# One stretch of turns, values and scores in a fused attention and recurrent-gate kernel

## The chip, the cores and the metric

The kernel runs on one core of a Trainium2 chip. The metric is device time in microseconds (us): 938.83 us, the median of 3 runs (937.73 to 939.91). The core's engines are TensorE (PE; its weight loads are PEld), VectorE (DVE), ScalarE (ACT), GpSimd (POOL) and SyncE (SP), which issues nearly all DMAs. Each works through its own list of instructions in order, and semaphores tie them together.

## The reference

The input x is 8 x 512 x 512, and so is the context. Two residual blocks follow each other:

```python
# block 1: windowed attention; queries = layernorm(x), keys = values = context
scores = einsum(q, k) / sqrt(32)          # 16 heads of 32
scores = where(|i - j| > 64, -inf, scores)
x = x + softmax(scores) @ v @ W_proj.T + b_proj
# block 2: a gated recurrence over the 8 batches, state of 512 x 512
f, i, g = sigmoid(x2 @ wf.T + c @ uf.T + bf), sigmoid(...), tanh(...)   # x2 = layernorm(x)
c = f * c + i * g
x = x + tanh(x2 @ wo.T + c_final @ uo.T + bo)
```

## The kernel before, in words

Rows are cut in 32 tiles of 128 (4 per batch; t is the tile's place in its batch, 0 to 3). A tile's 16 heads are 4 groups of 4, and one group of one tile is a slot: 128 slots. For a slot, TensorE computes scores (L753) into four PSUM banks `ps_a`, VectorE adds the mask and takes the row minimum (L1035, the mask step), ScalarE takes the exponential and its sum (L923), TensorE turns the part under the tile's own keys (L775) into a PSUM bank and ScalarE copies it out (L928, counted by `turned_a`), VectorE turns the sides in 32x32 blocks (L1070, step `sides`), and TensorE multiplies by the values (L796, L801) into `ps_v`. Edge tiles (t = 0 and 3) have half the sides.

Behind a tile's four slots come: `recip` (reciprocals of the sums, L1046), `send` (turned and sent through DRAM, L1051), `mult` (values by reciprocals, L1080), `halves` (split in a rounded part on ScalarE, L936, and a rest on GpSimd, L685), `proj` on TensorE into `ps_m` (L706 to L708), `resid` (L1085, empties `ps_m`), `stat2`, and `ln2b` (L1105). The normalised tile is turned for block 2: in tiles t = 3 by TensorE into `ps_m` (`turn2`, L843), in the others (`MOVED`, 18 tiles) by a DMA through DRAM and a block transpose on VectorE (`turn2`, L1111), with a rounded copy on ScalarE (`turn2_hi`, L945) and a rest on VectorE (`turn2_lo`, L1118). Queries of tiles from 11 on come as x_t by DMA (`load_q`, L580) and are normalised by VectorE in two operations (`query_norm`, L1025 and L1027).

Block 2's gate products are `cell`s: three matmuls of 128x512 each (L706 to L708 into `ps_g`), 8 cells to a unit. When a unit is whole, ScalarE takes its tanh (`gate`, L970), and VectorE blends it (L1142, L1156, L1159).

The order is one list, `steps`, written out by hand at L152 to L339; every engine walks through it and picks its own steps. From slot 36 on (`FIRST_TWO`) the slots go two by two: a double slot has two turns, 12 cells (2, 3 and 7), scores of the next two slots, and the values of its own two. Double slots with s = 0 also carry the projection of the tile before, and those with s = 2 the `mult` of their own. VectorE's `ln1` (L1003 to L1008) takes the statistics of tile i+2. Both turns go to `ps_a` banks, which is why the scores wait for both copies.

Of the kernel before, what the change touches and what calls it, by code (L numbers as in the profile page):

```python
# [20 lines left out]
def bass_xattn_ffn(nc, x, x_t, ctx_rows, ctx_t, w_proj, b_proj, w_gates, u_gates, biases, w_out, u_out, b_out, in_c,  # L21
# [143 lines left out]
    while cells_done < len(products):  # L165
        i, s = n // G, n % G
        if n >= FIRST_TWO:
            both = [m for m in (n, n + 1) if m < SLOTS]
            ahead = [m for m in (n + 2, n + 3) if m < SLOTS]
            steps.extend(("turn", m) for m in both)  # L170
            if s == 0:
                tile_steps("ln1", i + 2)
            cells(2)
# [6 lines left out]
            gates(2)  # L180
            steps.extend(("score", m) for m in ahead[:1])
            if s == 2 and i - 1 not in MOVED:
                tile_steps("turn2_lo", i - 1)
            steps.extend(("score", m) for m in ahead[1:])
            if s == 0:
# [6 lines left out]
            steps.extend(("exp", m) for m in ahead)  # L192
            steps.extend(("value", m) for m in both)
            if s == 0:
                tile_steps("proj", i - 1)
            else:
                tile_steps("mult", i)
            gates()
            renew()
            cells(3)  # L200
            steps.extend(("recip", m) for m in ahead[:1])
            if s == 0:
                tile_steps("resid", i - 1)
                tile_steps("stat2", i - 1)
            else:
                tile_steps("halves", i)
            steps.extend(("recip", m) for m in ahead[1:])
            if s == 0:
                tile_steps("send", i)
            steps.extend(("sides", m) for m in ahead[:1])  # L210
            if s == 0 and i + 1 >= TURNED_X:
                tile_steps("query_norm", i + 1)
            if s == 0 and i + 1 < TURNED_X:
                tile_steps("query", i + 1)
                tile_steps("query_out", i + 1)
            if s == 0 and i - 2 in MOVED:
                tile_steps("turn2", i - 2)
                tile_steps("turn2_hi", i - 2)
            gates()
            cells(7)  # L220
            if s == 0 and i - 1 not in MOVED:
                if i - 2 in MOVED:
                    tile_steps("turn2_lo", i - 2)
                tile_steps("ln2b", i - 1)
# [8 lines left out]
            gates(3)  # L233
            steps.extend(("sides", m) for m in ahead[1:])
            renew()
# [119 lines left out]
    with ExitStack() as ctx:  # L355
# [130 lines left out]
        x2t_home[0] = x2t_home[B - 2]  # L486
        ps_turn = [ps_g[0] if n < OWN_BANKS else ps_a[n % 2 if n >= FIRST_TWO else 0] for n in range(SLOTS)]

# [215 lines left out]
        def _(pe):  # L704
# [13 lines left out]
            for kind, i in steps:  # L718
# [14 lines left out]
                if kind == "score":  # L733
# [4 lines left out]
                    if i >= FIRST_TWO + 2:  # L738
                        pe.wait_ge(masked, HPG * (i - i % 2))
                        pe.wait_ge(turned_a, i - i % 2)  # L740
                    else:
                        need(pe, masked, HPG * i)
                        if i - 2 >= OWN_BANKS:
                            pe.wait_ge(turned_a, i - 1)
# [11 lines left out]
                if kind == "turn":  # L756
                    own = OWN0[i // G % TT]
                    if i < OWN_BANKS:
# [9 lines left out]
                        continue  # L768
                    if i >= FIRST_TWO:
                        pe.wait_ge(masked, HPG * (i - i % 2 + 2))  # L770
                    else:
                        pe.wait_ge(masked, HPG * (i + 1) + 1)
# [48 lines left out]
                if kind == "proj":  # L821
# [3 lines left out]
                    if i < WHOLE:  # L825
                        pe.wait_ge(attn_t, i + 1)
                        for k in range(G):
                            mm = pe.matmul(ps_m[:, :], attn[:, k, :], wp[:, k, :], start=(k == 0), stop=(k == G - 1))  # L828
                    else:
                        pe.wait_ge(wp_lo, G)  # L830
                        pe.wait_ge(attn_split, i - WHOLE + 1)
                        if i + 1 >= SENT:
                            pe.wait_ge(q_ready, min(i + 2, TURNED_X))
                        for k in range(G):
                            mm = product(ps_m[:, :], (attn_hi[:, k, :], attn_lo[:, k, :]),
                                         (proj_w[:, 0, k, :], proj_w[:, 1, k, :]), k == 0, k == G - 1)
                    mm.then_inc(projected, 1)
                if kind == "turn2" and i not in MOVED:
                    pe.wait_ge(x2_done, i + 1)
                    need(pe, q_ready, min(i + 3, TURNED_X))  # L840
                    need(pe, column_turned, len([n for n in row_at if n < G * (i + 1) + 2]))
                    for k in range(G):
                        mm = pe.transpose(ps_m[:, k * P:(k + 1) * P], x2[:, k * P:(k + 1) * P], ident[:, :])  # L843
# [59 lines left out]
        def _(act):  # L903
# [4 lines left out]
            for kind, i in steps:  # L908
# [16 lines left out]
                if kind == "turn":  # L925
                    act.wait_ge(turned, i + 1)
                    need(act, valued, i - i % 2 if i >= FIRST_TWO else i)
                    act.activation(own_home[i], ps_turn[i][:, :].rearrange("p (a q) -> p a q", a=HPG), ACT.Copy)\  # L928
# [65 lines left out]
        def _(dve):  # L994
# [4 lines left out]
            for kind, i in steps:  # L999
# [21 lines left out]
                if kind == "query_norm":  # L1021
# [5 lines left out]
                    dve.tensor_tensor(queries[:, :, :], queries[:, :, :], rstd, ALU.mult).then_inc(q_ready, 1)  # L1027
                if kind == "score":
                    t = i // G % TT
# [28 lines left out]
                if kind == "sides":  # L1058
                    dve.wait_ge(expd, HPG * (i + 1))
                    dve.wait_ge(valued, i - i % 2 if i >= FIRST_TWO else i)  # L1060

# [180 lines left out]
```

## Time and profile before

| | |
|---|---|
| median of 3 runs | 938.83 us (937.73 to 939.91) |
| profiled execution | 939.05 us, of which the span 937.2 |
| TensorE busy | 920.3 us, 98% of the span |
| VectorE busy | 674.9 us, 72% |
| ScalarE busy | 476.7 us, 51% |
| GpSimd busy | 206.0 us, 22% |
| granted TensorE clock, mean | 0.998 |

The table is read from the profile's first part. Busy time is the time in which an engine executes, without its waits; ends of matmuls are modelled, so on TensorE the distances between starts say more than the durations.

### The profile page before, as it was taken

The numbers are of one execution on the slowest core, as the hardware profiler recorded it, in microseconds if no ns is written. First come the engines' busy times: TensorE is split into PE (matmuls) and PEld (weight loads), VectorE is DVE, ScalarE is ACT, GpSimd is POOL, SyncE is SP. The second block draws the span as 40 slices with busy tenths as digits, with TensorE's granted clock in tenths as the row PEclk, the third lists the DMA queues.
The fourth block names the chain that finished last, engine by engine and source line by source line (L and its number), as shares of the span: only waits on it lengthen the run. The fifth ranks groups of instructions, "written<-read, shape, count | busy, mean of one in ns | idle before, by whom it ended". The sixth has DMA issues, their size and how long they took to land.

```text
span 937.2 us, 21983 instructions
## 1 busy us (share of the span) xinstructions
PE 920.3 (98%) x7842; PEld 716.2 (76%) x7842; DVE 674.9 (72%) x2275; ACT 476.7 (51%) x1430; POOL 206.0 (22%) x236
## 2 busy tenths in 40 slices
PE   7999899999999999999999999999999999999998
PEld 5555567677887788878787888788877888888887
DVE  6888987888779977997799878987798531143222
ACT  6888666655555544555465555555555321131222
POOL 5576322211111111111111111111101100003444
PEclk9999999999999999999999999999999999999999
DMA  9564223224443443434543444344333150059862
GB/s 303 165 200 145 86 80 108 87 69 130 132 139 112 130 132 92 143 108 129 133 141 109 119 116 125 108 109 109 98 99 92 50 164 0 1 178 384 316 233 101
DMA packets 139348, 123.58 MB, mean 132 GB/s; under 512 B 46824, under 2 KB 104168, under 8 KB 137704
## 3 DMA queue, kind: packets, MB, share of 16 engines
q1 hardware_dynamic: 138520, 121.91, 42.9%
q8 instruction: 63, 1.03, 0.5%
q10 hardware_dynamic: 720, 0.27, 0.2%
q14 instruction: 45, 0.37, 0.1%
HBM read 87.70 MB, written 34.46 MB: 130 GB/s over the span
## 4 chain that ended last, share of the span: by engine, by line
PE 89%; DVE 5%; ACT 2%; issue 2%; DMA 1%; SPq 0%; DVEq 0%; ACTq 0%
PE ps_g L706 18%; PE ps_g L708 18%; PE ps_g L707 18%; PE ps_a L753 5%; PE ps_a L775 5%; PE ps_m L706 3%; PE ps_v L796 3%; PE ps_m L708 3%; PE ps_m L707 3%; PE ps_m L828 2%; PE ps_a L708 2%; PE ps_a L706 2%; PE ps_a L707 2%; ACT probs L923 2%; PE ps_v L801 2%
## 5 line engine op out<-in xcount | busy, mean ns | idle before, releaser
L923 ACT ACTIVATE probs<-probs,rowmin 128x192 f32<-128x192 f32 (+1 forms) x512 | 239.4, 470 | 114.0 <-DVE rowmin L1035 114.0
L1035 DVE CUSTOM_DVE_ANT_0 probs<-ps_a,mask 128x192 f32<-128x192 f32 (+1 forms) x512 | 166.1, 386 | 28.4 <-PE ps_a L753 26.8
L706 PE MATMUL ps_g<-state_hi,gate_w 128*128 128x512 f32 x336 | 133.6, 398 | 0.0
L708 PE MATMUL ps_g<-state_hi,gate_w 128*128 128x512 f32 x336 | 131.1, 390 | 0.0
L707 PE MATMUL ps_g<-state_lo,gate_w 128*128 128x512 f32 x336 | 130.8, 389 | 0.0
L1070 DVE STREAM_TRANSPOSE keys<-probs 32x128 f32<-32x128 f32 x420 | 125.5, 299 | 5.6 <-issue 0.2
L970 ACT ACTIVATE gate<-ps_g,bias 128x512 f32<-128x512 f32 x84 | 57.6, 686 | 105.8 <-PE ps_g L708 105.1
L923 ACT ACTIVATION_READ_ACCUMULATOR probs<-probs,rowmin 128x1 f32 x512 | 96.4, 188 | 0.0
L928 ACT ACTIVATE probs_t<-ps_a 128x512 f32<-128x512 f32 x108 | 59.3, 595 | 61.1 <-PE ps_a L775 61.1
L685 POOL TENSOR_TENSOR attn_lo<-recip,attn_hi 128x512 fp32r<-128x512 f32 x23 | 29.7, 1292 | 275.8 <-ACT attn_hi L936 275.8
L706 PE MATMUL ps_g<-x2t_even,gate_w 128*128 128x512 f32 x192 | 80.5, 419 | 0.0
L706 PE MATMUL ps_g<-x2t_odd,gate_w 128*128 128x512 f32 x192 | 76.9, 401 | 0.0
L708 PE MATMUL ps_g<-x2t_even,gate_w 128*128 128x512 f32 x192 | 75.6, 394 | 0.0
L707 PE MATMUL ps_g<-x2t_even,gate_w 128*128 128x512 f32 x192 | 75.5, 393 | 0.0
L708 PE MATMUL ps_g<-x2t_odd,gate_w 128*128 128x512 f32 x192 | 74.9, 390 | 0.0
L707 PE MATMUL ps_g<-x2t_odd,gate_w 128*128 128x512 f32 x192 | 74.8, 390 | 0.0
L708 PEld LDWEIGHTS ps_g<-state_hi,gate_w 128*128 128x128 f32 x336 | 63.1, 188 | 13.5
L706 PEld LDWEIGHTS ps_g<-state_hi,gate_w 128*128 128x128 f32 x336 | 63.1, 188 | 12.6
L707 PEld LDWEIGHTS ps_g<-state_lo,gate_w 128*128 128x128 f32 x336 | 63.2, 188 | 12.3
L753 PE MATMUL ps_a<-keys,queries 32*64 32x192 f32 (+1 forms) x2048 | 62.7, 326 | 2.4 <-DVE rowmin L1035 1.9
L775 PE MATMUL ps_a<-ident,probs 128*128 128x128 f32 x432 | 60.5, 274 | 2.2 <-ACT probs L923 0.8
L775 PEld LDWEIGHTS ps_a<-ident,probs 128*128 128x128 f32 x432 | 51.1, 139 | 14.4 <-ACT probs L923 4.2
(220 smaller groups left out, 1723.5 us busy)
## 6 DMA issues: line engine op xcount, KB each, us to landing
values<-ctx_rows SPq DMA_DIRECT2D x34, 256.0 KB, 4.4
xr<-x SPq DMA_DIRECT2D x32, 256.0 KB, 3.8
keys<-ctx_t SPq DMA_DIRECT2D x16, 512.0 KB, 4.2
x_dram<-xr SPq DMA_DIRECT2D x32, 256.0 KB, 2.6
gate_w<-x2t_dram SPq DMA_DIRECT2D x8, 1024.0 KB, 10.1
keys<-ctx_t SPq DMA_DIRECT2D x16, 384.0 KB, 3.4
x2t_dram<-x2t_even SPq DMA_DIRECT2D x12, 512.0 KB, 4.4
x2t_dram<-x2t_odd SPq DMA_DIRECT2D x12, 512.0 KB, 4.5
```

What stands on the lines that cost most here:

```text
L685: pool.tensor_tensor(attn_lo[:, :, :], attn if i < SENT else recip[:, :, :], attn_hi[:, :, :].bitcast(F32), ALU.subtract)\
L706: pe.matmul(ps, lhs[0], rhs[0], start=start, stop=False)
L707: pe.matmul(ps, lhs[0], rhs[1], start=False, stop=False)
L708: return pe.matmul(ps, lhs[1], rhs[0], start=False, stop=stop)
L753: mm = pe.matmul(ps_a[h][q, score_at[i] + k.start:score_at[i] + k.stop], queries[rows, g, q], keys[rows, key_home[tile], g, k], start=True ...
L775: mm = pe.transpose(ps_turn[i][:, h * P:(h + 1) * P], probs[:, i % 2, h, own:own + P], ident[:, :])
L796: pe.matmul(ps_v[HEAD * h:HEAD * (h + 1), g * P:(g + 1) * P], values[:, tile % 2, 0, d], own_home[i][:, h, :], start=True, stop=False)
L923: act.activation(row, row, ACT.Exp, bias=rowmin[:, i % 2, h:h + 1], scale=-1.0, accum_out=rowsum[:, i // G % 2, i % G, h:h + 1]).then_inc( ...
L928: act.activation(own_home[i], ps_turn[i][:, :].rearrange("p (a q) -> p a q", a=HPG), ACT.Copy)\
L970: act.activation(gate[:, min(gt, 1), :], ps_g[i % 2][:, :], ACT.Tanh, bias=(first_bias if b == 0 else bias)[:, gt, m:m + 1], scale=1.0 if ...
L1035: dve.tensor_tensor_reduce(probs[:, i % 2, h, 0:SEEN[t]], ps_a[h][:, score_at[i]:score_at[i] + SEEN[t]], mask[:, MASK0[t]:MASK0[t] + SEEN[ ...
L1070: turn = dve.transpose(side_home[i][BLK * keys_of:BLK * (keys_of + 1), :, q], probs[q, i % 2, :, col:col + BLK])
```

## The change

From slot 36 on, TensorE's order in a double slot n, n+1 is: turn n, values n-2 and n-1, turn n+1, scores n+2 and n+3, and then the cells; before it was both turns, 2 cells, scores, values, 10 cells. Values come one double slot later than before. Odd turns go to `ps_m` in place of `ps_a[1]`, with waits for what else uses that bank; the scores wait only for the first turn's copy. On VectorE, scores' masks are a step of their own (`mask`), behind both `sides`; `query_norm` follows, then `ln1`, `recip`, `resid`, `stat2`, `send` and the `turn2` of a moved tile. `mult` and `halves` of a tile move to the start of the next double slot, the projection behind 5 cells, and the `query` of tile 10 behind all cells.

```diff
             both = [m for m in (n, n + 1) if m < SLOTS]
             ahead = [m for m in (n + 2, n + 3) if m < SLOTS]
-            steps.extend(("turn", m) for m in both)
-            if s == 0:
-                tile_steps("ln1", i + 2)
+            back = [m for m in (n - 2, n - 1) if FIRST_TWO <= m < SLOTS]
+            steps.extend(("turn", m) for m in both[:1])
+            steps.extend(("value", m) for m in back)
+            steps.extend(("turn", m) for m in both[1:])
+            steps.extend(("score", m) for m in ahead)
+            if s == 0 and i - 1 >= SENT:
+                tile_steps("mult", i - 1)
+                tile_steps("halves", i - 1)
+            late_sides = [m for m in both if m >= FIRST_TWO + 2]
+            steps.extend(("sides", m) for m in late_sides[:1])
             cells(2)
...
             gates(2)
-            steps.extend(("score", m) for m in ahead[:1])
+            steps.extend(("sides", m) for m in late_sides[1:])
             if s == 2 and i - 1 not in MOVED:
                 tile_steps("turn2_lo", i - 1)
-            steps.extend(("score", m) for m in ahead[1:])
+            steps.extend(("mask", m) for m in ahead)
...
             steps.extend(("exp", m) for m in ahead)
-            steps.extend(("value", m) for m in both)
-            if s == 0:
-                tile_steps("proj", i - 1)
-            else:
-                tile_steps("mult", i)
             gates()
             renew()
             cells(3)
-            steps.extend(("recip", m) for m in ahead[:1])
             if s == 0:
+                tile_steps("proj", i - 1)
+            gates()
+            if s == 0 and i + 1 >= TURNED_X:
+                tile_steps("query_norm", i + 1)
+            if s == 0:
+                tile_steps("ln1", i + 2)
+                steps.extend(("recip", m) for m in ahead)
                 tile_steps("resid", i - 1)
                 tile_steps("stat2", i - 1)
-            else:
-                tile_steps("halves", i)
-            steps.extend(("recip", m) for m in ahead[1:])
-            if s == 0:
                 tile_steps("send", i)
-            steps.extend(("sides", m) for m in ahead[:1])
-            if s == 0 and i + 1 >= TURNED_X:
-                tile_steps("query_norm", i + 1)
-            if s == 0 and i + 1 < TURNED_X:
-                tile_steps("query", i + 1)
-                tile_steps("query_out", i + 1)
             if s == 0 and i - 2 in MOVED:
                 tile_steps("turn2", i - 2)
                 tile_steps("turn2_hi", i - 2)
             gates()
             cells(7)
+            if s == 0 and i + 1 < TURNED_X:
+                tile_steps("query", i + 1)
+                tile_steps("query_out", i + 1)
...
             gates(3)
-            steps.extend(("sides", m) for m in ahead[1:])
+            if s == 2:
+                steps.extend(("recip", m) for m in ahead)
...
-        ps_turn = [ps_g[0] if n < OWN_BANKS else ps_a[n % 2 if n >= FIRST_TWO else 0] for n in range(SLOTS)]
+        ps_turn = [ps_g[0] if n < OWN_BANKS else ps_m if n >= FIRST_TWO and n % 2 else ps_a[0] for n in range(SLOTS)]
...  # TensorE, score
-                        pe.wait_ge(turned_a, i - i % 2)
+                        pe.wait_ge(turned_a, i - i % 2 - 1)
...  # TensorE, turn
+                        tile = i // G
                         pe.wait_ge(masked, HPG * (i - i % 2 + 2))
+                        if i % 2:
+                            pe.wait_ge(recip_out, SENT)
+                            pe.wait_ge(x1_done, tile - 1 + (i % G) // 2)
+                            pe.wait_ge(x2_lo, split_by(tile - 1))
+                            pe.wait_ge(q_ready, min(tile + 1 + (i % G) // 2, TURNED_X))
...  # TensorE, proj; turn2 has the same with + 4
+                            pe.wait_ge(turned_a, min(G * (i + 1) + 2, SLOTS))
...  # ScalarE, turn; VectorE, sides has the same
-                    need(act, valued, i - i % 2 if i >= FIRST_TWO else i)
+                    need(act, valued, i - 1 if i >= FIRST_TWO + 2 else i - i % 2 if i >= FIRST_TWO else i)
...  # VectorE
-                if kind == "score":
+                if kind == ("mask" if isinstance(i, int) and i >= FIRST_TWO + 2 else "score"):
```

## Rows read from the trace of the kernel before

**Rows 1.** Stretches view: engines' busy us and instructions, granted clock, DMA share, GB/s
```profile
195.00:730.00 535.00, 535.00 (x4921) 429.15 (x4920) 448.98 (x1538) 286.97 (x902) 83.07 (x84) 1.00 0.42 117
```
**Rows 2.** Timeline, TensorE: start, us, engine, line, operation, count; three stretches
```profile
505.07 1.03 PE L775 MATMUL ps_a<-ident,probs 128*128 128x128 f32 x8
...
519.03 1.03 PE L775 MATMUL ps_a<-ident,probs 128*128 128x128 f32 x8
519.82 0.48 PE L706 MATMUL ps_g<-x2t_even,gate_w 128*128 128x512 f32 x1
520.14 0.40 PE L707 MATMUL ps_g<-x2t_even,gate_w 128*128 128x512 f32 x1
...
521.05 0.39 PE L708 MATMUL ps_g<-x2t_even,gate_w 128*128 128x512 f32 x1
521.37 0.88 PE L753 MATMUL ps_a<-keys,queries 32*64 32x192 f32 x32
522.18 0.43 PE L796 MATMUL ps_v<-probs_t,values 128*32 128x128 f32 x8
...
523.19 0.50 PE L706 MATMUL ps_g<-x2t_even,gate_w 128*128 128x512 f32 x1
523.53 0.40 PE L707 MATMUL ps_g<-x2t_even,gate_w 128*128 128x512 f32 x1
...
554.71 1.03 PE L775 MATMUL ps_a<-ident,probs 128*128 128x128 f32 x8
...
568.37 1.03 PE L775 MATMUL ps_a<-ident,probs 128*128 128x128 f32 x8
```
**Rows 3.** Timeline, TensorE, before the double slots: turns ahead of values and of scores
```profile
72.08 0.66 PE L819 MATMUL ps_m<-ident,recip 128*128 128x128 f32 x4
72.66 0.78 PE L789 MATMUL ps_v<-probs_t,values 128*32 128x128 f32 x16
...
124.59 0.60 PE L731 MATMUL ps_m<-ident,tile_row 128*128 128x128 f32 x4
125.12 0.58 PE L753 MATMUL ps_a<-keys,queries 32*64 32x192 f32 x16
```
**Rows 4.** The load of x_t: DMA view, VectorE's waits (total, times, longest), two timelines
```profile
queries<-x_t SPq DMA_DIRECT2D x21, 256.0 KB, 4.3
...
DVE queries L1025 <- DMA queries<-x_t: 4.3, 7, 1.3
...
561.26 0.58 SPq L580 DMA_DIRECT2D queries<-x_t  x1
...
565.54 0.69 DVE L1025 TENSOR_TENSOR queries<-queries,tile_row 128x512 f32<-128x512 f32 x1 [0.60 <-DMA queries<-x_t]
```
**Rows 5.** Timeline, VectorE, in the double slot that starts at 505.07
```profile
508.68 0.69 DVE L1003 BATCH_NORM_STATS2 st<-xr 128x6 f32<-128x512 f32 x1
...
509.77 0.42 DVE L1035 CUSTOM_DVE_ANT_0 probs<-ps_a,mask 128x256 f32<-128x256 f32 x1
...
512.63 0.66 DVE L1085 TENSOR_TENSOR xr<-ps_m,xr 128x512 f32<-128x512 f32 x1
...
514.39 0.18 DVE L1046 RECIPROCAL invsum<-rowsum 128x4 f32<-128x4 f32 x1
...
514.74 1.84 DVE L1070 STREAM_TRANSPOSE keys<-probs 32x128 f32<-32x128 f32 x6
516.61 0.69 DVE L1025 TENSOR_TENSOR queries<-queries,tile_row 128x512 f32<-128x512 f32 x1
...
518.14 0.71 DVE L1111 STREAM_TRANSPOSE tile_row<-x2t_odd 128x512 f32<-128x512 f32 x1
```
**Rows 6.** Timeline, ScalarE, around the next turns
```profile
518.89 0.63 ACT L945 ACTIVATE x2t_odd<-tile_row 128x512 fp32r<-128x512 f32 x1 [3.96 <-DVE tile_row L1111]
519.43 0.67 ACT L970 ACTIVATE gate<-ps_g,bias 128x512 f32<-128x512 f32 x1
520.00 1.08 ACT L928 ACTIVATE probs_t<-ps_a 128x512 f32<-128x512 f32 x2
```

More of the change, by code:

```diff
@@ L841, in _ @@
                     need(pe, column_turned, len([n for n in row_at if n < G * (i + 1) + 2]))
+                    if i + 1 >= SENT:
+                        pe.wait_ge(turned_a, min(G * (i + 1) + 4, SLOTS))
                     for k in range(G):
@@ L1059, in _ @@
                     dve.wait_ge(expd, HPG * (i + 1))
-                    dve.wait_ge(valued, i - i % 2 if i >= FIRST_TWO else i)
+                    dve.wait_ge(valued, i - 1 if i >= FIRST_TWO + 2 else i - i % 2 if i >= FIRST_TWO else i)
                     if i == OWN_BANKS:
```

## The prediction

> **What bounds the kernel now.** I read the stretch view first, over the part of the span in which attention and the gate products run together in double slots: between 195 and 730 us TensorE is busy for all 535.00 us at a granted clock of 1.00 (its higher level, 2.4 GHz), VectorE for 449, ScalarE for 287 and GpSimd for 83 [rows 1]. So no wait of TensorE is there to be taken away; the time can fall only if TensorE starts its next group sooner, and it rises with every wait that is new. Then I read TensorE in order of time through one double slot [rows 2]. Only starts are used, since the ends are modelled: a gate product is three matmuls, each starting 0.227 us after the one before. I call the start of a double slot's first turn T0. Last I followed VectorE and ScalarE through the double slots that carry a projection (s = 0, below called A; the one after it, s = 2, is B) [rows 4 to 6], since 449 of 535 us is close to full for an engine that works strictly in the order written.
>
> **TensorE's own time.** The profiled double slot B has 36 gate matmuls, 36 x 0.227 = 8.17 us. The rest: eight turns 0.79 and the next matmul's longer first gap (0.32 instead of 0.23) 0.09; the gap ahead of the scores 0.32 instead of 0.23, so 0.09; 32 score instructions 0.81; the two slots' values 1.01; the first gap after them 0.34, so 0.11. Sum 2.90 us [rows 2]. Eight turns with the entry of what follows are 0.88, or 0.11 a turn: breaking the gate products for turns costs next to nothing.
>
> After the change the order is turn, values, values, turn, scores. Four turns ahead of values took 0.58 us, four ahead of scores 0.53 [rows 3]; against 4 x 0.11 = 0.44 that is 0.14 and 0.09 more. Values again 1.01, scores 0.81; what follows the scores is now a gate matmul, which the trace never shows; by its nearest rows its first gap is longer by 0.09 to 0.11 [rows 2], and the turn behind the values by as much. Sum 0.58 + 1.01 + 0.10 + 0.53 + 0.81 + 0.10 = 3.13 us, 0.2 more than before. Bounds: if a turn is as cheap ahead of values and scores as ahead of gate products (0.44 for four) and values cost the turn behind them nothing, the sum is 0.44 + 1.01 + 0.44 + 0.81 + 0.09 = 2.79 and the change gains 0.11 a double slot; if each of the two edges never seen (values to turn, scores to gate matmul) costs what the gap ahead of the scores and the one after values do together, 0.2, the sum is 3.33 and it loses 0.43. Near the middle but towards the cheap side I take a loss of 0.13, for 45 double slots (first slots 36 to 124) 6 us, range -5 to +19.
>
> The Trainium skill, TensorEngine Tiling (Array Packing), Key Properties, says that a change of tiling mode drains TensorE. Turns and gate products are both full 128x128, so by it there were three mode changes in a double slot (to scores, to values, back) and will be four (values, back to a turn, scores, back): the fewer stretches hold more drains. At 0.09 to 0.2 each that alone would be 4 to 9 us slower. The trace agrees in that the turn next to gate products is the one edge that is nearly free [rows 2].
>
> **The queue behind the queries.** Here is the large term. In A VectorE now does: `mult`, both `sides`, eight masks, `query_norm`, then `ln1`, two `recip`, `resid`, `stat2`, `send`, and only then VectorE's `turn2` of tile i-2. ScalarE's copy of it (`turn2_hi`) stands ahead of the gate that ends with A's last cell, and that ahead of the copy of B's first turn; and B's scores wait for that copy (`turned_a`), because they overwrite its bank. Before, `turn2` stood right behind `query_norm`, and the scores came two gate products later.
>
> `query_norm` can't come earlier, because x_t isn't there: its load is issued once the last scores of the tile are done, 4.9 to 6.5 us behind T0 in the trace (561.26 - 554.71 = 6.55 in the one shown) and lands a median 4.3 us later; VectorE stood waiting for it in 7 of 21 tiles, and in the one shown, with t=0, began at T0 + 10.83 [rows 2, 4]. The new order ends A's scores at T0 + 3.1, where they end now, so the landing stays: T0 + 10.9 for t=0, where one more value load is issued ahead of it, and for the others the request at 4.9 to 5.5 plus 4.3 and a little: some 9.8 for t=3 and 9.7 for t=2 (estimates). VectorE is free before that: `mult` from T0 + 1.9, sides 2 x 1.9, masks 2.8, so T0 + 9.2 at the latest.
> From the start of `query_norm`: until its successor starts 1.53; `ln1` 1.09; one `recip` 0.2 (estimate); `resid` and `stat2` 514.39 - 512.63 = 1.76; the other `recip` and `send` 0.35; so `turn2` starts 4.9 us behind it instead of 1.53 [rows 5]. From its start: ScalarE's copy after 0.75, gate after 1.29, the turn's copy after 1.86 and done at 2.4 to 2.5 [rows 5, 6]. Together 7.4 us from `query_norm` to the bank being free.
> When B's scores are due: A took 519.03 - 505.07 = 13.96 (t=2) and 568.37 - 554.71 = 13.66 (t=0) [rows 2], plus 0.13; the scores follow 0.6 + 1.0 + 0.6 = 2.2 behind that, at T0 + 16.3 and T0 + 16.0 (15.8 where an edge tile's short side values save 0.2, estimate).
> So the wait is 10.9 + 7.4 - 15.8 = 2.5 us at t=0 (5 tiles), 9.8 + 7.4 - 15.8 = 1.4 at t=3 (5), 9.7 + 7.4 - 16.3 = 0.8 at t=2 (6), none at t=1, whose tile i-2 is turned by TensorE. 12.5 + 7.0 + 4.8 = 24 us; I take 23, as t=2 is often nearer nothing. The bounds are 0 (should ScalarE or the load be 2 us earlier than laid out) and 40 (a microsecond more in each of 16). TensorE has no slack elsewhere to win it back.
>
> **Edits that I cost at nothing.** Odd turns go to `ps_m` and wait for `resid`, done at `query_norm` + 3.4, T0 + 13.2 to 14.3, while the turn is due at T0 + 15.6; where that cover is gone it costs what is missing. `mult` of a tile comes one double slot later and its halves are ready near T0 + 5; the projection has five gate products ahead of it now and starts at T0 + 3.1 + 3.4 = 6.5. The masks of A start near T0 + 6.5 instead of 4.7 and the exponentials end by T0 + 11, due at the next turn, T0 + 14; in B they end near its end, with 1 to 2 us to spare for the second turn. If that is gone too, each A loses about 1 us. SyncE: keys, values and x_t are requested at the same offsets; the tile's store and the send come 1 to 2 us later, in front of loads that are needed a double slot on. The later query of tile 10 happens once: under 1 us either way. Values a double slot later use sides and copies that are long done.
>
> Sum against the profiled execution's 939.05 us (span 937.2 and 1.85 around it): 939.05 + 23 + 6 = 968.05. It stands 0.22 above the median 938.83, so 967.8 us.
>
> **Rivals.** (1) The queue is not late, only the edges count: 939 + 6 = 945. For it: VectorE has 86 us idle in the stretch; against it: x_t's landing was already waited for. 20%. (2) The other side: the single stretch lets weight loads run ahead across edges, each double slot gains 0.11, as in the lower bound, and `turn2` is in time because masks and sides are out of the way: 939 - 45 x 0.11 = 934. It decides if a double slot's attention takes under 2.90 us on TensorE and x_t lands before T0 + 8.4. For it: two breaks of the gate products become one; against it: rows 2 to 4. 8%. (3) Both the queue and a second wait: in B the masks, behind two sides, let ScalarE's exponentials reach past T0 and push gate and copy in A too; 22 times 0.5 us more: 979. 14%. (4) It comes to nothing, edges cheaper and waits small: 939. 5%. The forecast, 23 us of waits and 6 of edges, has 53%, its own range 955 to 975.
>
> Slower by over 0.2% (about what can be told from no change here) is the forecast, rivals 1 and 3, and nothing else: 87%; same 4%, faster 9%. Range: from 943 (rival 1 inside) to 981 (rival 3 inside).
>
> **What would show it.** Right: TensorE idle ahead of the scores in B with ScalarE's `probs_t` copy as what ended it, about 2.5, 1.4 and 0.8 us at t=0, 3, 2 and nothing at t=1; VectorE idle ahead of L1025 for x_t in nearly every tile; in an unwaited double slot 3.0 to 3.1 us between gate products. Wrong: no TensorE idle between 195 and 750 us, or idle ahead of the turns instead of the scores; a stretch under 2.9 us.

## The result, and the profile after

The changed kernel takes 983.5 us, the median of 4 runs (982.62 to 988.8), against 938.7 us for the kernel before (4 runs, 937.73 to 939.91). The ratio is 1.0488, with a 95% interval of 1.0449 to 1.0528. The forecast was 967.8 us with a range up to 981: the direction is right, the time lies 2.5 us above the range. The profiled execution took 983.95 us with a span of 982.0 us, and the granted clock had a mean of 0.984 (before: 0.998).

The first part of the page after, and the chain of waits by engine (share of the span):

```profile
PE 940.0 (96%) x7842; PEld 730.1 (74%) x7842; DVE 652.5 (66%) x2275; ACT 477.3 (49%) x1430; POOL 199.9 (20%) x236
...
PE 59%; DVE 15%; DMA 11%; SPq 7%; issue 4%; ACT 4%; POOL 0%; ACTq 0%; DVEq 0%
```

Before, TensorE held the chain nearly alone; now 41% of it runs over other engines, the DMAs and SyncE's queue (SPq). The stretches view of after has first the whole part with double slots, then a piece of one B (t = 2), the one in the timeline below:

```profile
195.00:780.00 585.00, 558.56 (x4987) 445.44 (x4978) 433.12 (x1567) 289.76 (x912) 75.78 (x83) 0.98 0.39 107
...
548.90:552.90 4.00, 4.00 (x14) 3.13 (x11) 3.90 (x20) 1.32 (x6) 0.00 (x0) 0.50 0.87 266
```

TensorE was busy for every microsecond of the stretch of before [rows 1]; it is idle for 26.4 of these 585 us. The second line runs at half clock (0.50, which is 1.2 GHz); from 553.20 on the clock is 1.00 (2.4 GHz) again. The waits view (total us, times, longest) names what TensorE, VectorE and SyncE waited for in the same part:

```profile
PE ps_a L755 <- ACT probs_t L939: 26.0, 15, 2.9
DVE queries L1036 <- DMA queries<-x_t: 50.3, 18, 5.0
...
SPq L503 <- DMA x_dram<-tile_row: 50.7, 16, 5.1
```

The first line is the wait that was forecast: scores behind ScalarE's copy of the first turn. The second is VectorE's wait for x_t, 4.3 us in 7 times before [rows 4]. The last is SyncE waiting for the store of x2 to land.

TensorE in order of time (start, us, line, operation, count): the end of an A without a wait, and the B that follows it, with one.

```profile
527.78 0.60 PE L783 MATMUL ps_a<-ident,probs 128*128 128x128 f32 x4
528.32 0.43 PE L804 MATMUL ps_v<-probs_t,values 128*32 128x128 f32 x8
529.33 0.66 PE L783 MATMUL ps_m<-ident,probs 128*128 128x128 f32 x4
529.91 0.91 PE L755 MATMUL ps_a<-keys,queries 32*64 32x192 f32 x32
530.75 0.50 PE L708 MATMUL ps_g<-state_hi,gate_w 128*128 128x512 f32 x1
...
541.79 0.60 PE L783 MATMUL ps_a<-ident,probs 128*128 128x128 f32 x4
543.82 0.63 PE L783 MATMUL ps_m<-ident,probs 128*128 128x128 f32 x4 [0.42 <-issue]
547.39 1.56 PE L755 MATMUL ps_a<-keys,queries 32*64 32x192 f32 x32 [2.94 <-ACT probs_t L939]
548.88 0.80 PE L708 MATMUL ps_g<-x2t_even,gate_w 128*128 128x512 f32 x1
549.47 0.63 PE L709 MATMUL ps_g<-x2t_even,gate_w 128*128 128x512 f32 x1
549.90 0.63 PE L710 MATMUL ps_g<-x2t_even,gate_w 128*128 128x512 f32 x1
```

In A (527.78) the five groups stand close together: 0.54 + 1.01 + 0.58 + 0.84, and then a first gate gap of some 0.34. In B the scores start at 547.39, after 2.94 us idle. Behind that wait the 32 score instructions take 1.49 us in place of 0.84, and up to about 552.9 the matmuls start 0.43 us apart in place of 0.227.

**Where 44.8 us went.** From the start of the second double slot (206.05 us before, 205.10 after) to one and the same gate matmul behind the last (777.04 and 822.0) the trace of before has 570.99 us and that of after 616.9, so 45.9 us lie there; ahead of it after is 1 us quicker. They come apart like this: 26.4 us of idle time, 26.0 of it ahead of the scores of 15 double slots and 0.4 ahead of one second turn; 11.9 us in 7 stretches at half clock (8.2 of it in gate matmuls, 3.0 in scores, 0.6 in the rest, each taken against the same distance between starts at full clock); and what is left, 7.6 us, which I put down to the edges, 0.17 in each of 44 double slots. The starts in double slots without a wait give the same 0.17 by themselves: on average 0.53 + 0.61 for the turns, 0.83 for the scores and 0.11 for the longer first gate gap, 2.08 us, where before it was 0.79 + 0.09 + 0.09 + 0.83 + 0.11 = 1.91; the values are alike.

**Why ScalarE's copy is late.** VectorE and ScalarE in the double slots of the fence above (T0 of A is 527.78):

```profile
539.96 0.69 DVE L1036 TENSOR_TENSOR queries<-queries,tile_row 128x512 f32<-128x512 f32 x1 [2.82 <-DMA queries<-x_t]
...
544.84 0.68 DVE L1122 STREAM_TRANSPOSE tile_row<-x2t_odd 128x512 f32<-128x512 f32 x1
545.55 0.63 ACT L956 ACTIVATE x2t_odd<-tile_row 128x512 fp32r<-128x512 f32 x1 [6.11 <-DVE tile_row L1122]
546.09 0.67 ACT L981 ACTIVATE gate<-ps_g,bias 128x512 f32<-128x512 f32 x1
546.66 0.59 ACT L939 ACTIVATE probs_t<-ps_a 128x512 f32<-128x512 f32 x1
```

This is the chain of the prediction: from `query_norm` to `turn2` 4.88 us (forecast 4.9, before 1.53 [rows 5]), copy after 0.71, gate after 1.25, the turn's copy after 1.82. What was not forecast is where it starts: 539.96 is T0 + 12.18, laid out for t = 2 at T0 + 9.7.

**Why x_t is late.** The chain of waits from 516 to 549 us, in order of time (start, us, what), leads back over SyncE:

```profile
520.46 0.56 SPq L572
521.07 5.67 DMA x_dram<-tile_row
526.88 0.32 SPq L579
...
533.38 1.24 SPq L526
...
535.77 4.16 DMA queries<-x_t
539.96 0.70 DVE queries L1036
```

L572 reads the reciprocals back, the DMA `x_dram<-tile_row` is the store of x2, L579 fetches the norm rows, L562 the four blocks of x2, L526 to L536 keys and values. The same steps of before and then of after, as SyncE's timeline has them:

```profile
493.79 0.56 SPq L570 DMA_DIRECT2D recip<-recip_dram  x1
497.38 0.33 SPq L551 DMA_DIRECT2D x_dram<-tile_row  x1
499.62 0.80 SPq L577 DMA_DIRECT2D tile_row<-recip_dram  x2
500.54 4.83 SPq L560 DMA_DIRECT2D x2t_odd<-x_dram  x4
508.41 0.39 SPq L524 DMA_DIRECT2D keys<-ctx_t  x1
509.96 0.58 SPq L580 DMA_DIRECT2D queries<-x_t  x1
```

```profile
520.46 0.56 SPq L572 DMA_DIRECT2D recip<-recip_dram  x1
521.07 0.47 SPq L553 DMA_DIRECT2D x_dram<-tile_row  x1
...
526.88 1.68 SPq L579 DMA_DIRECT2D tile_row<-recip_dram  x2
528.67 4.66 SPq L562 DMA_DIRECT2D x2t_odd<-x_dram  x4
533.38 1.24 SPq L526 DMA_DIRECT2D keys<-ctx_t  x1
535.77 0.58 SPq L582 DMA_DIRECT2D queries<-x_t  x1
```

Before, the store was issued 3.6 us behind the read back, and the norm rows followed it after 2.2 us, well ahead of the next A (T0 = 505.07); x_t was requested at T0 + 4.9. After, the store is issued 0.6 us behind the read back and the norm rows wait 5.8 us for it, to T0 - 0.9; the four fetches then stand in the queue until T0 + 5.6, ahead of the keys, and x_t is requested at T0 + 8.0. So there is a chain: `send` comes late, because it now stands behind `query_norm`, `ln1`, `recip`, `resid` and `stat2`; that puts the read back right ahead of the store; the store lands late; the fetches reach into the next A; x_t is requested late; `query_norm` is late. In t = 2 x_t was requested at T0 + 7.0 to 8.0 from the second batch on (5.2 in the first); in t = 3 (4.7 to 5.5) and t = 0 (5.3 to 6.1) it was not, or hardly, later than before.

Where the late `query_norm` makes the next `send` late in its turn, the chain closes to a ring, and the expectations below call it one. In after it does not get round. At t = 1, ahead of which no x2 is stored and fetched, x_t was requested at T0 + 5.1 to 5.9 and VectorE waited for it 0.4 us at most; the order of its own steps is enough to put the next store 0.6 us behind the read back. So the delay starts anew in each batch.

### The profile page after: what moved, and what is told of

The parts are those of the page before. It is cut to its first block, busy times and chain, and to the rows that moved or that the text cites. A ratio compares the mean times of both kernels' runs of the same rounds, so it can differ in the third digit from the quotient of the medians.

```text
span 982.0 us, 22081 instructions
## 1 busy us (share of the span) xinstructions
PE 940.0 (96%) x7842; PEld 730.1 (74%) x7842; DVE 652.5 (66%) x2275; ACT 477.3 (49%) x1430; POOL 199.9 (20%) x236
## 4 chain that ended last, share of the span: by engine, by line
PE 59%; DVE 15%; DMA 11%; SPq 7%; issue 4%; ACT 4%; POOL 0%; ACTq 0%; DVEq 0%
PE ps_g L708 12%; PE ps_g L710 11%; PE ps_g L709 11%; DMA queries<-x_t 7%; PE ps_a L755 4%; DMA x_dram<-tile_row 3%; SPq L562 3%; DVE probs L1046 2%; ACT probs L934 2%; PE ps_m L836 2%; PE ps_a L708 2%; PE ps_a L709 2%; PE ps_a L710 2%; PE ps_v L804 2%; PE ps_a L783 2%
## 5 line engine op out<-in xcount | busy, mean ns | idle before, releaser
L708 PE MATMUL ps_g<-state_hi,gate_w 128*128 128x512 f32 x336 | 135.5, 403 | 0.0
L710 PE MATMUL ps_g<-state_hi,gate_w 128*128 128x512 f32 x336 | 132.1, 393 | 0.0
L755 PE MATMUL ps_a<-keys,queries 32*64 32x192 f32 (+1 forms) x2048 | 66.3, 340 | 27.8 <-ACT probs_t L939 26.3
L708 PE MATMUL ps_g<-x2t_even,gate_w 128*128 128x512 f32 x192 | 81.3, 424 | 0.0
L710 PE MATMUL ps_g<-x2t_even,gate_w 128*128 128x512 f32 x192 | 76.8, 400 | 0.0
L709 PE MATMUL ps_g<-x2t_even,gate_w 128*128 128x512 f32 x192 | 76.7, 399 | 0.0
L1167 DVE SCALAR_TENSOR_TENSOR gate<-gate,state 128x512 f32<-128x512 f32 x28 | 19.4, 692 | 76.9 <-ACT gate L981 76.9
L755 PEld LDWEIGHTS ps_a<-keys,queries 32*64 32x64 f32 x2048 | 36.2, 136 | 44.6 <-issue 42.2
L939 ACT ACTIVATE probs_t<-ps_a 128x512 f32<-128x512 f32 x62 | 36.8, 594 | 55.2 <-PE ps_v L809 39.1
```

The lines of the kernel that those rows point to most:

```text
L708: pe.matmul(ps, lhs[0], rhs[0], start=start, stop=False)
L709: pe.matmul(ps, lhs[0], rhs[1], start=False, stop=False)
L710: return pe.matmul(ps, lhs[1], rhs[0], start=False, stop=stop)
L755: mm = pe.matmul(ps_a[h][q, score_at[i] + k.start:score_at[i] + k.stop], queries[rows, g, q], keys[rows, key_home[tile], g, k], start=True ...
```

## The experiments

Each was timed beside the kernel before on the same chip, whose median was 939.08 us beside the first four, 938.9 beside the next four and 938.38 beside the last. Waits are totals over the part with double slots, 195 to 780 us of the profiled execution. The experiments stand in the order in which they ran. Where an expectation speaks of e1, e6 or e8, it means "turn2 directly behind the queries", "statistics and send ahead of the queries" and "the queue without the single stretch".

**turn2 directly behind the queries.** Both steps of tile i-2 move to right behind `query_norm`, as in the kernel before; all else as after.

```diff
             if s == 0 and i + 1 >= TURNED_X:
                 tile_steps("query_norm", i + 1)
+            if s == 0 and i - 2 in MOVED:
+                tile_steps("turn2", i - 2)
+                tile_steps("turn2_hi", i - 2)
             if s == 0:
                 tile_steps("ln1", i + 2)
...
                 tile_steps("send", i)
-            if s == 0 and i - 2 in MOVED:
-                tile_steps("turn2", i - 2)
-                tile_steps("turn2_hi", i - 2)
```

> The changed kernel with VectorE's and ScalarE's turn of tile i-2 right behind the normalising of the queries, ahead of ln1, recip, resid, stat2 and send. Queue theory (26 us of TensorE waits, 12 us at half clock and 7 to 8 us of edges make the 45 us): the turn starts some 3.3 us sooner, every wait ahead of the scores but perhaps some tenths at t=2 goes, and the half-clock stretches with them; 944 to 949 us. Rival, the wait is for exponentials or gates that ScalarE does late, whatever VectorE's turn does: TensorE still waits about 2 us in B, 975 to 984 us. Rival, the half clock has a cause of its own: waits go, the clock still falls 7 times, 956 to 960 us.

Measured: 982.29 us (977.78 to 983.51), ratio 1.0445 [1.0413, 1.0476]. The expectation failed. Its waits:

```profile
PE ps_m L783 <- issue: 26.4, 13, 3.6
...
DVE queries L1036 <- DMA queries<-x_t: 74.8, 16, 7.5
```

The wait ahead of the scores falls to 3.4 us, but the second turn now waits as long for its bank `ps_m`, which `resid` empties: `ln1`, `recip` and `resid` stand behind the same late `query_norm`. VectorE waited 74.8 us for x_t, and from the second batch on x_t was requested at T0 + 6.6 to 9.4 in three tiles of four, but at 5.7 to 6.7 in t = 1. Here the delay does go on from tile to tile, t = 2, 3 and 0, and ends at t = 1. In this run the order behind `query_norm` only chose which step was late. Time and size of the waits are as the expectation's first rival had them, but they stand at the second turn, and not for the reason that it gave.

**Only ScalarE's copy later.** `turn2` stays where the change put it; its copy `turn2_hi` moves behind the scores of the next double slot (at t = 0 with the two steps that need it).

```diff
             steps.extend(("score", m) for m in ahead)
+            if s == 2 and i - 2 in MOVED:
+                tile_steps("turn2_hi", i - 2)
...  # at t = 0, turn2_lo and ln2b move too
             if s == 0 and i - 2 in MOVED:
                 tile_steps("turn2", i - 2)
-                tile_steps("turn2_hi", i - 2)
...
```

> The changed kernel with VectorE's order of the s = 0 double slot up to its turn of tile i-2 untouched; only ScalarE's rounded copy of that turn comes behind the next double slot's turn copies (and, at t=0, VectorE's rest and ln2b with it). Queue theory: the late turn reaches TensorE only through ScalarE's strict order, so the waits ahead of the scores go although VectorE is as late as before; 944 to 950 us. Rival, VectorE's own lateness holds TensorE (through sides, masks or resid): waits stay above 15 us in all, over 965 us.

Measured: 967.14 us (963.82 to 970.03), 1.0294 [1.0265, 1.0323].

```profile
PE ps_m L783 <- issue: 15.0, 10, 2.8
```

The waits for the copy fall from 26.0 to 2.5 us, so the link from `turn2` over ScalarE's order to the scores is shown. It is not the whole cause: x_t stays late (VectorE waited 72.3 us for it), 15 us of waits come back at the second turn and 3.2 at TensorE's own `turn2`. The time and the waits (20.7 us in all) are those of the expectation's rival: VectorE's lateness holds TensorE by another step, `resid`. The profiled execution, 970.03 us, was the slowest of the four.

**TensorE kept busy in the wait.** Sixteen turns of the identity into a free part of `ps_a[3]` ahead of the wait, in B of t = 0 and 2 (11 times).

```diff
                         pe.wait_ge(masked, HPG * (i - i % 2))
+                        if i % 4 == 0 and (i // G - 1) % TT in (0, 2):
+                            for _ in range(16):
+                                pe.transpose(ps_a[3][:, 0:P], ident[:, :], ident[:, :])
                         pe.wait_ge(turned_a, i - i % 2 - 1)
```

> The changed kernel with 16 transposes of the identity (about 1.7 us) on TensorE ahead of its wait for the turn's copy, in the B double slots of t=0 and t=2 only (11 of them); they go to a score bank that the scores overwrite. The wait for the copy itself stays. Clock theory (TensorE's idle of over 2 us is what lets the granted clock fall for some 3 to 4 us after it): idle shrinks to under 1.3 us, no stretch at 0.43 us a matmul is left, and the kernel gets 8 to 12 us faster than the changed one although it does more: 971 to 977 us. Rival (the clock falls for another reason, or the fill delays the scores one for one): 983 us or more.

Measured: 976.09 us (973.84 to 976.64), 1.0385 [1.037, 1.0401], as expected. The stretches line, and one place in order of time:

```profile
195.00:780.00 585.00, 572.32 (x5174) 461.59 (x5160) 434.64 (x1571) 291.53 (x921) 76.39 (x84) 1.00 0.40 107
```

```profile
272.46 1.91 PE L744 MATMUL ps_a<-ident 128*128 128x128 f32 x16
275.13 0.91 PE L758 MATMUL ps_a<-keys,queries 32*64 32x192 f32 x32 [0.76 <-ACT probs_t L942]
```

No stretch at half clock is left (1.00, after: 0.98), though the scores start no earlier: work that computes nothing made the kernel 7.4 us faster. Eleven fillers of 1.84 us (16 turns between 219.95 and 221.79 us, where the scores behind them had nothing to wait for) are 20.2 us; the waits for the copy fell by less, from 26.0 to 10.7 us, and the second turn's rose by 1.5. So 4.9 + 1.5 + 7.4 = 13.8 us came back from the clock, against 11.9 counted in the trace of after. The half clock is a term of its own.

**The queue without the single stretch.** The kernel before, TensorE's order untouched; `ln1`, `resid`, `stat2` and `send` go between `query_norm` and `turn2`.

```diff
-            if s == 0:
-                tile_steps("ln1", i + 2)
             cells(2)
...
-                tile_steps("resid", i - 1)
-                tile_steps("stat2", i - 1)
...
-                tile_steps("send", i)
             steps.extend(("sides", m) for m in ahead[:1])
             if s == 0 and i + 1 >= TURNED_X:
                 tile_steps("query_norm", i + 1)
+            if s == 0:
+                tile_steps("ln1", i + 2)
+                tile_steps("resid", i - 1)
+                tile_steps("stat2", i - 1)
+                tile_steps("send", i)
```

> The kernel before with one part of the change: VectorE's ln1, resid, stat2 and send stand between the normalising of the queries and the turn of tile i-2; TensorE's order is that of before, so there is no new edge. Queue theory: in B the turn's two copies are late for the scores by about 2.3 us at t=0, 1 at t=3 and 0.5 at t=2, some 16 to 20 us, and a few us of half clock where a wait passes 2 us: 955 to 966 us. Rival, the long stretch on TensorE is what makes the change slow: within 2 us of before, 937 to 941 us.

Measured: 988.23 us (984.91 to 989.67), 1.0514 [1.0491, 1.0538]: more than was expected, and as much as the whole change.

```profile
PE ps_a L751 <- ACT probs_t L926: 13.7, 10, 1.9
PE ps_m L841 <- DVE tile_row L1103: 11.5, 5, 2.9
PE ps_v L794 <- DVE keys L1068: 8.3, 7, 1.7
```

The single stretch is not needed for the loss. The waits fall at other places, because other steps follow in that order, and x_t is requested as late (T0 + 6.6 to 8.9 in t = 2 from the second batch on). Five stretches at half clock come with them.

**Statistics and send ahead of the queries.** After, with `ln1` at the head of A, and `recip`, `resid`, `stat2`, `recip`, `send` ahead of `query_norm` instead of behind it.

```diff
             steps.extend(("score", m) for m in ahead)
+            if s == 0:
+                tile_steps("ln1", i + 2)
...
-            if s == 0 and i + 1 >= TURNED_X:
-                tile_steps("query_norm", i + 1)
             if s == 0:
-                tile_steps("ln1", i + 2)
-                steps.extend(("recip", m) for m in ahead)
+                steps.extend(("recip", m) for m in ahead[:1])
                 tile_steps("resid", i - 1)
                 tile_steps("stat2", i - 1)
+                steps.extend(("recip", m) for m in ahead[1:])
                 tile_steps("send", i)
+            if s == 0 and i + 1 >= TURNED_X:
+                tile_steps("query_norm", i + 1)
```

> The changed kernel, TensorE's stretch and all, with VectorE's order behind the masks put back as before: recip, resid, stat2, recip, send and only then query_norm and the turn of tile i-2 (ln1 stands at the head of the double slot). Ring theory (e1 and e8 made me form it: what stands behind query_norm waits for x_t; send late puts its read back on top of the x2 store, the store lands 5 us instead of 2.5 later, the fetch behind it on SyncE holds up the loads of keys and x_t, and query_norm is later still): TensorE has under 3 us of waits from 195 to 780 us, x_t is requested within 6.5 us of the double slot's start in every tile, and only the edges of the stretch are left; 944 to 950 us. Rival, the masks behind two sides (ScalarE's exponentials late) are a cause of their own: more than 10 us of waits, 960 us or more.

Measured: 960.76 us (959.84 to 961.25), 1.0235 [1.0221, 1.0249], the fastest version of the change.

```profile
PE ps_a L757 <- ACT probs_t L941: 12.1, 15, 1.3
PE ps_m L710 <- issue: 2.5, 5, 0.5
...
DVE xr L1098 <- PE ps_m L712: 27.5, 11, 2.6
```

The chain over SyncE is gone: the store of x2 lands in 2.7 us (median), x_t is requested at T0 + 4.7 to 6.0 in every tile, VectorE never waits for it, and the clock is 1.00 everywhere. The expected 944 to 950 was missed because `resid` now waits for the projection (27.5 us of VectorE's time; 33.1 with one more wait of 5.6 behind this part), and `query_norm` and `turn2` stand behind it. Time and waits are as the rival had them, masks and exponentials late; the last experiment decides between the two. 960.8 - 938.9 = 21.9 is 14.6 of waits and a rest of 7.3, the edges.

**Both turns together.** The same, with turn, turn, values, values, scores.

```diff
             steps.extend(("turn", m) for m in both[:1])
-            steps.extend(("value", m) for m in back)
             steps.extend(("turn", m) for m in both[1:])
+            steps.extend(("value", m) for m in back)
```

> As e6, with both turns ahead of the values: turn, turn, values, values, scores. One change of the array's shape fewer in a double slot (turns to values, values to scores, scores to gate products). Edge theory: each change costs 0.1 to 0.2 us, so a double slot takes 2.9 us on TensorE in place of 3.08 and this is 4 to 8 us faster than e6, near the kernel before: 938 to 942 us. Rival, the edges hardly depend on the order, or values to scores is dear: within 2 us of e6.

Measured: 966.46 us (966.37 to 967.37), 1.0299 [1.0285, 1.0313].

```profile
PE ps_a L756 <- ACT probs_t L940: 25.2, 44, 0.8
```

A new small wait stands in all 44 double slots: the first turn's copy has to wait for the values that read its home in `probs_t`, and these now come behind both turns. What is left without it is 966.5 - 938.9 - 25.2 = 2.4 us of edges, against 7.3; the starts give 0.06 a double slot over the kernel before, against 0.17. So one array change fewer (turns to values to scores to gate products, three in place of four) is worth up to 5 us, 0.11 a double slot. It is an upper figure: the new wait stands at the change from values to scores in every double slot and can hide part of its price. The time itself was missed. Whether a third home for the copies would take the wait away, no run shows.

**The read back behind the store.** After, with the second DMA of `send` (the reciprocals read back) issued behind the store of x2 and the next x.

```diff
+                if kind == "send_back":
                     sp.wait_ge(recip_sent, DMA * (sent + 1))
...
                 tile_steps("load_x", i + 3)
+                if i >= SENT:
+                    tile_steps("send_back", i)
```

> The changed kernel with one DMA moved on SyncE: the read of the reciprocals from DRAM comes behind the x2 store and the load of x of the next double slot, in place of right ahead of them. Ring theory: the x2 store lands some 2.5 us after its issue again (4.9 in the changed kernel), the fetch ends 2 to 3 us sooner, x_t is requested at T0 + 5 to 6 at t=2 (7 to 8 now), and the waits ahead of the scores at t=2 fall from 2 to under 1 us, with most half-clock stretches: 962 to 974 us. Rival, the slow landing has nothing to do with the read back (or SyncE's lateness does not matter): 980 to 985 us.

Measured: 975.82 us (971.9 to 979.72), 1.0397 [1.0369, 1.0424], just above what was expected. The profiled execution was the slowest, 979.72 us, so its waits are on the high side. The DMA view's row for the store of x2 (count, KB, median us from issue to landing) in after, and then in this kernel (before: 2.5):

```profile
x_dram<-tile_row SPq DMA_DIRECT2D x16, 256.0 KB, 4.9
```

```profile
x_dram<-tile_row SPq DMA_DIRECT2D x16, 256.0 KB, 2.0
```

The store lands in 2.0 us again, x_t of t = 2 is requested at T0 + 4.7 to 5.7, and the wait there falls to 0.6 us or nothing. That link of the chain is shown. The time is not regained in full: in four of the five tiles t = 3 the fetches now end about T0 + 4 and x_t is requested at 6.3 to 6.7, so 22.7 us of waits remain, 2.3 to 2.9 each in those four, and six stretches at half clock.

**The fetches behind the loads.** After, with the four fetches of x2 issued behind the next A's keys, values and x_t.

```diff
-                if i - 1 in MOVED:
-                    tile_steps("fetch_x2", i - 1)
...
                 if i + 1 >= TURNED_X:
                     tile_steps("load_q", i + 1)
+                if i - 2 in MOVED:
+                    tile_steps("fetch_x2", i - 2)
```

> The changed kernel with the four fetches of the moved tile behind the next double slot's loads of keys, values and x_t on SyncE. Ring theory: keys and x_t are requested at T0 + 3.1 and 5 in every tile, so the waits at t=2 fall to some 0.8 us; the waits at t=0 stay unless the fetch, now later, lands behind VectorE's turn, due at T0 + 15; 965 to 976 us. Rival, the fetch lands too late and takes the place of x_t as what VectorE waits for: 983 us or more.

Measured: 964.18 us (962.32 to 970.28), 1.0284 [1.0254, 1.0314].

```profile
PE ps_a L755 <- ACT probs_t L939: 14.6, 14, 2.0
```

The chain is cut at another link: the store still lands in 5.5 to 6.0 us where it is issued 0.6 us behind the read back, but keys are requested at T0 + 3.1 and x_t at T0 + 4.7 to 6.1 in every tile. 983.5 - 964.2 = 19 us came from SyncE's order alone, with VectorE's and TensorE's order of after untouched. It has two parts: 11.8 us fewer waits, and two stretches at half clock in place of seven, 3.2 us in place of 11.9. The 14.6 us of waits that stay are the ones behind `query_norm` that were forecast, without the lateness from SyncE: on average 1.7 us at t = 0, 0.6 at t = 3, 0.5 at t = 2.

**Projection earlier.** The kernel with statistics first, its projection behind 3 cells instead of 5.

```diff
-            cells(3)
+            cells(1)
             if s == 0:
                 tile_steps("proj", i - 1)
+            cells(2)
```

> As e6, with the projection behind 3 of the 12 gate products instead of 5. In e6 VectorE stood 33 us in all ahead of resid for the projection, so query_norm began at T0 + 12.4 at t=2 though x_t had landed, and TensorE still waited 14.6 us. Ring theory in its last form: with resid 1.36 us sooner the normalising and the turn come sooner too, TensorE's waits fall under 5 us, the clock stays at 1.00, and what is left is the edges alone, 45 double slots at 0.14 to 0.16 us, 6 to 7 us: 945 to 950 us. Rival, the waits of e6 come from the masks and exponentials: still 958 us or more.

Measured: 969.01 us (968.72 to 970.93), 1.0329 [1.0315, 1.0343], slower than its parent by 8 us.

```profile
PE ps_m L711 <- issue: 11.8, 15, 1.9
PE ps_a L758 <- ACT probs_t L942: 1.7, 6, 0.3
```

The scores' waits fall from 12.1 to 1.7 us with the masks left where they were, so they did come from `resid` behind the projection, and not from masks and exponentials. But the projection now waits 11.8 us for the `halves` (GpSimd writes the rest up to right before it), and four of its waits of 1.9 us, at t = 1, were followed by 3.4 us at half clock, 1.6 us lost each. Waits and half clock together explain some 5 of the 8 us; the rest stays open. In this layout both ends of the projection are tight.

No version came below the kernel before, and no run had the single stretch without any wait, so 939 + 8 = 947 us for that is worked out, not measured.

## Why the prediction was wrong, step by step

**The step that failed** is among the edits costed at nothing: "SyncE: keys, values and x_t are requested at the same offsets; the tile's store and the send come 1 to 2 us later, in front of loads that are needed a double slot on." At t = 2 x_t was requested up to 3 us later, the keys 2.3. I counted the instructions that were moved past loads, but not that the store's landing is itself waited for on SyncE (L579 and the fetches behind it), nor that it lands later when the read back is issued right ahead of it. Both cuts, on SyncE alone, show its price: 7.7 us (read back later, which made t = 3 late instead) and 19.3 us (fetches later). With the second the kernel takes 964.2 us, inside the range. The 19.3 holds most of the half clock, so the two terms of this section don't add.

**The half clock** was missing from the sum: 11.9 us, shown by the filler, and alone enough to carry the time over the range. Before, TensorE never waited in the double slots. But ahead of them the trace of before has one such stretch, behind 1.0 us of waits between 112.9 and 115.0 (us busy and instructions of PE, PEld, DVE, ACT and POOL, then the granted clock):

```profile
115.20:118.60 3.40, 3.40 (x23) 1.84 (x22) 2.82 (x8) 3.10 (x11) 1.56 (x2) 0.50 0.00 0
```

The gate matmuls in it start 0.43 us apart. This row would have priced the term: half of 3.4 us, 1.7, for each wait that brings it on.

**Waits ahead of B's scores**: forecast 23 us, measured 26.0. The sum is near by luck, its shares are not: at t = 0 2.3 on average (forecast 2.5), at t = 3 0.5 (1.4), at t = 1 none (none), at t = 2 2.0 (0.8). t = 2, expected to be "often nearer nothing", is where SyncE is late. Without that lateness the forecast chain cost 14.6 us (fetches behind the loads), so by itself it was forecast too high. Its links behind `query_norm`, 4.9 and then 2.4 to 2.5 us, held to 0.1 us in the tile shown.

**Edges**: forecast 0.13 in 45 double slots, 6 us (the rows added up to 0.23, and 0.13 was taken); measured 0.17 in 44, 7.6 us. The parts moved against each other, on average: turn ahead of values 0.53 (0.58), turn ahead of scores 0.61 (0.53), scores and the first gate gap 0.83 + 0.11 over 0.227 (0.81 + 0.10), and nothing between the values and the start of the turn behind them (0.10), unless the 0.08 by which that turn is longer is this change's price. The Trainium skill, TensorEngine Tiling (Array Packing), Key Properties, says that changing the tiling mode drains TensorE, and gives no time. The trace agrees as far as it goes: four changes of array shape in place of three cost 0.17 us more a double slot, and with three again, in another order, it was 0.06.

**Odd turns' wait for `resid`** had the cover that was claimed in after (waits of 0.42 us at most there), and lost it as soon as `turn2` went ahead of `ln1` (26.4 us). **`mult`, `halves` and the projection** held: no wait in after; with two cells less the cover is gone. **Rival 3**, masks and exponentials late in A, did not occur, although its 979 us is nearer to the result than the forecast, and no wait stands ahead of A's scores; nearness to a wrong mechanism proves nothing. **Rival 1** (edges only) would need the queue to be in time, which no version reached.

Open: what decides which wait is followed by half clock. In after waits of 2.09 and 2.12 us were; with the projection earlier four of 1.9 us were and a fifth was not; with the read back later one of 1.8 was, and waits of 2.29 and 2.37 us were not. Length alone does not settle it, and no run here does.

## What to carry to other kernels

Where a step that waits for a load is put ahead of others, follow two lists: what stands behind it on its own engine, and what its lateness does to the queue that issues the next such load; if they close, the delay goes on from one load to the next. Here it could be cut on either side: on SyncE (fetches behind the loads) or on VectorE (statistics and `send` ahead of the queries). Price a new wait on TensorE of some 2 us with the half clock too, here 1.7 us for each of 7 waits out of 15. And count changes of array shape, not breaks, before work is merged in one stretch.

## What the runs showed of the hardware

- The store of x2 (256 KB) landed 5.5 to 6.0 us after its issue when it was issued 0.6 us behind the read back of the reciprocals (after, t = 2 from the second batch on), 2.0 to 3.7 us when 2.2 to 5.2 us behind it (before; median 2.5), and 2.0 us (median) when issued ahead of it (read back later). The median of all tiles of after is 4.9.
- At 7 of 15 waits ahead of scores in after (2.09 to 2.94 us) the granted clock fell from 1.00 to 0.50, six times for 3.4 us and once for 6.8, 1.3 of it within the wait, and matmuls of 128x512 started 0.43 us apart instead of 0.227: 1.5 to 2.6 us lost each. The other eight waits were of 0.3 to 1.95 us. Turns of the identity in the wait kept it at 1.00.
- Sixteen turns of 128x128 in a row took 1.84 us, 0.115 each, the same as the 0.11 worked out for turns between gate products.
